# A transformer layer in fp32: the down projection of two steps as seven products of half the columns

## What is computed

```
x = fwht(x * SU_ug) / SCALE                      # Hadamard transform over 512
x_up   = x @ W_up.T   * (Wscale_ug[:INTER] * SCALE)     # 512 -> 2048
x_gate = x @ W_gate.T * (Wscale_ug[INTER:] * SCALE)
x = silu(x_gate) * x_up
x = fwht(x * SU_dp) / SCALE
x = x @ W_down.T * (Wscale_dp * SCALE)           # 2048 -> 512, "down"
x = layernorm(x_in + x)
```

## Time and profile before

| | |
|---|---|
| median of 3 runs | 1549.19 us |
| profiled execution | 1548.87 us, span 1547.1 us |
| granted clock of TensorE, mean | 0.998 |
| PE matmuls | 11744, busy 98% |
| VectorE (DVE), ScalarE (ACT), GpSimd (POOL) busy | 67%, 40%, 30% |
| attention / block 0 / blocks 1 to 7 / end | 0 to 510 / 510 to 661 / 661 to 1530 / to 1547 us |

### The profile page before, as it was taken

How to read it: one execution, slowest core, us unless ns; L and a number is a source line. 1 busy time by engine, 2 the same in 40 slices (tenths; PEclk the granted TensorE clock), 3 DMA queues, 4 the chain that set the end, 5 groups by cost and what they waited for, 6 DMA issues and landing times.

```text
span 1547.1 us, 29636 instructions
## 1 busy us (share of the span) xinstructions
PE 1513.5 (98%) x11744; PEld 1422.1 (92%) x11744; DVE 1034.0 (67%) x1790; ACT 625.8 (40%) x1289; POOL 465.0 (30%) x580
## 2 busy tenths in 40 slices
PE   6999999999999999999999999999999999999998
PEld 5977978888887899899999999999999999999998
DVE  6876787677687886865575576566467547557645
ACT  4263245236227755533333343343343333334332
POOL 5465457438338533500220030030040022003001
PEclk9999999999999999999999999999999999999999
DMA  7031122122112796678578667767776857866862
GB/s 284 1 116 69 35 83 102 35 82 103 64 64 101 275 378 246 236 273 307 205 242 295 231 241 263 268 216 264 272 238 226 322 195 257 288 231 231 283 234 97
DMA packets 92072, 307.63 MB, mean 199 GB/s; under 512 B 9888, under 2 KB 10272, under 8 KB 90144
## 3 DMA queue, kind: packets, MB, share of 16 engines
q1 hardware_dynamic: 90928, 301.54, 54.8%
q10 hardware_dynamic: 1008, 4.20, 0.7%
HBM read 255.37 MB, written 50.33 MB: 198 GB/s over the span
## 4 chain that ended last, share of the span: by engine, by line
PE 64%; DVE 4%; ACT 1%; issue 1%; POOL 1%; POOLq 0%; DVEq 0%; ACTq 0%
PE ff_bank_b L2061 16%; PE ff_bank_a L2061 11%; PE ff_bank_c L2061 11%; PE ff_acc L2095 8%; PE ff_acc L2098 7%; PE ff_acc L2086 7%; DVE ff_d_lo L1775 2%; PE ff_x_ps L2020 1%; PE ff_x_ps L2009 1%; PE ff_x_ps L2032 1%; ACT at_union L601 1%; DVE ff_c L1826 0%; DVE ff_h_lo L1794 0%; DVE ff_c L1822 0%; DVE ff_ring L1770 0%
## 5 line engine op out<-in xcount | busy, mean ns | idle before, releaser
L2061 PE MATMUL ff_bank_b<-ff_x_hi,ff_ring 128*128 128x256 f32 x1536 | 296.8, 278 | 4.1 <-DVE ff_c L1826 3.5
L2061 PEld LDWEIGHTS ff_bank_b<-ff_x_hi,ff_ring 128*128 128x128 f32 x1536 | 246.3, 188 | 5.6 <-issue 5.4
L2061 PE MATMUL ff_bank_b<-ff_x_lo,ff_ring 128*128 128x256 f32 x768 | 212.8, 277 | 0.0
L2095 PE MATMUL ff_acc<-ff_d_lo,ff_h_hi 128*128 128x256 f32 x1008 | 199.8, 279 | 2.4 <-DVE ff_d_lo L1775 2.4
L2061 PE MATMUL ff_bank_c<-ff_x_hi,ff_ring 128*128 128x256 f32 x1024 | 200.3, 280 | 0.0
L2061 PE MATMUL ff_bank_a<-ff_x_hi,ff_ring 128*128 128x256 f32 x1024 | 199.6, 279 | 0.0
L2098 PE MATMUL ff_acc<-ff_d_hi,ff_h_lo 128*128 128x256 f32 x1008 | 197.7, 277 | 0.0
L2061 PEld LDWEIGHTS ff_bank_c<-ff_x_hi,ff_ring 128*128 128x128 f32 x1024 | 164.2, 188 | 2.2 <-issue 2.2
L2061 PEld LDWEIGHTS ff_bank_a<-ff_x_hi,ff_ring 128*128 128x128 f32 x1024 | 164.3, 188 | 0.3 <-issue 0.2
L1822 DVE TENSOR_TENSOR ff_c<-ff_bank_b,ff_c 128x512 f32<-128x512 f32 x64 | 44.3, 692 | 172.0 <-PE ff_bank_b L2061 171.1
L2095 PEld LDWEIGHTS ff_acc<-ff_d_lo,ff_h_hi 128*128 128x128 f32 x1008 | 152.9, 188 | 6.4 <-issue 6.4
(11 more groups left out here) (321 smaller groups left out, 3482.3 us busy)
## 6 DMA issues: line engine op xcount, KB each, us to landing
ff_ring<-gu_scratch SPq DMA_DIRECT2D x392, 512.0 KB, 5.1
gu_scratch<-ff_ring SPq DMA_DIRECT2D x56, 512.0 KB, 4.3
at_xt<-in_xt SPq DMA_DIRECT2D x4, 2048.0 KB, 8.0
at_xn<-in_x SPq DMA_DIRECT2D x32, 256.0 KB, 2.9
x_scratch<-at_x SPq DMA_DIRECT2D x32, 256.0 KB, 2.0
ff_raw<-in_wgu SPq DMA_DIRECT2D x8, 1024.0 KB, 7.1
at_wd_a<-in_wd SPq DMA_DIRECT2D x8, 512.0 KB, 4.0
mixed_scratch<-at_wd_a SPq DMA_DIRECT2D x8, 512.0 KB, 3.3
```

Source lines behind the costliest of these rows:

```text
L2061: i = pe.matmul(bank[:, m, :], r[:, a, m, c, :], b[:, k, c, :], start=(k < 3 and m == 0 and c == 0 and b is x_hi and a == 0), stop=(m == 1 ...
L2095: pe.matmul(acc[:, t, half], h_hi[q][:, j, k], d_lo[:, j, half], start=False, stop=False, skip_group_check=True)
```

## The change

Two steps (four chunks of 128) are taken together, and the down product of them is done by Strassen-Winograd as well: h is cut into halves of tokens and odd and even chunks, `wd` into halves of its columns and odd and even chunks. Seven products (`down_product`) of 256 tokens x 256 columns x 256 inner values have 12 matmuls of 256 columns each, 84 for two steps. This holds for blocks 1 to 7 without the last two steps: `GROUPS` = 27 groups. Block 0 and the last two steps keep the old way (`whole`).

- PE: after the products of an even step p come the seven down products of the two steps before p (group q, `group_at`). After an odd step nothing comes. The banks 0, 1, 2 of `acc` are used in the order 0, 1, 2, 1, 0, 1, 2.
- The sum over the block is no longer in PSUM but in `y`: VectorE adds six times per group a bank to a quarter of y (`add_down`); product 1 (M1) is copied by ScalarE (`copy_m1`), summed over the groups by POOL (`add_m1`, not for a block's first group) and added to three quarters of y at the block's end (`close_y`).
- Tokens: POOL makes four sums of 256 elements per step (`sum_h`); ScalarE rounds and VectorE lowers four parts of h per step (`split_h`, `lower_part`), three of 512 elements and one of 256, two of them in the next step, before `product` 1.
- Weights: POOL combines the down weights once, 16 operations (`combine_down`). In each group ScalarE rounds seven operands (`split_pair`), POOL lowers five (`lower_pair`, three of them ahead), VectorE two. They share three slots.
- Statistics are taken in two parts in step 1 (`measure`). `X_AT` is moved, in part into the group (positions 12 and 15, behind down products 3 and 6). The fetch of y is issued two products after the store (n = 20, not 22). Tiles move in SBUF, some share space with those of block 0.

The core of the diff:

```diff
+        BANK_OF = (0, 1, 2, 1, 0, 1, 2)
+        READS = ((1, 0, 1), (2, 1, 1), (3, 1, 1), (4, 0, 0), (5, 1, 0), (6, 0, 1))
-        X_AT = {(4, 3): ("turn", 0), (4, 6): ("mix", 0), (4, 8): ("turn", 1), (5, 3): ("mix", 1), (5, 6): ("turn", 2),
-                (5, 8): ("mix", 2), (6, 3): ("turn", 3), (6, 6): ("mix", 3)}
+        X_AT = {(3, 6): ("turn", 0), (4, 3): ("mix", 0), (4, 6): ("turn", 1), (4, 12): ("mix", 1), (4, 15): ("turn", 2),
+                (5, 3): ("mix", 2), (5, 6): ("turn", 3), (6, 3): ("mix", 3)}
...
-                    if n == MULS * 3 + 1 and not last:
+                    if n == MULS * 2 + 6 and not last:
# POOL
+            def combine_down(g):
+                upper, lower = slice(4 * g, 4 * g + 3, 2), slice(4 * g + 1, 4 * g + 4, 2)
+                b11, b12, b21, b22 = (down_half(b, chunks) for chunks in (upper, lower) for b in range(2))
...
+            def sum_h(blk, p):
...
+                pool.wait_ge(*prod_s.now(s, 3))
+                pool.tensor_tensor(s1, a21, a22, ALU.add).then_inc(sum_s, 1)
+                pool.tensor_tensor(s3, a11, a21, ALU.subtract).then_inc(sum_s, 1)
...
+            def lower_pair(q, k):
+                n = MULS * q + k
+                pool.wait_ge(*pair_hi(n + 1))
+                pool.tensor_tensor(pair_slot(n, 1), pair_weights(q, k), pair_slot(n, 0).bitcast(F32), ALU.subtract).then_inc(b_lo, 1)
+
+            def lower_three(q):
+                for k in range(3):
+                    lower_pair(q, k)
+
+            def add_m1(q):
+                blk, g = q // 4 + 1, q % 4
+                if g == 0:
+                    return
+                pool.wait_ge(m1_copied, q + 1)
+                if g > 1:
+                    pool.wait_ge(*m1_added(blk, g - 1))
+                pool.tensor_tensor(m1_sum[:, :, :], m1_sum[:, :, :], m1[:, :, :], ALU.add).then_inc(m1_summed, 1)
+
+            def close_y(q):
...
+                for a, b, reads in ((1, 0, 0), (0, 1, 1), (1, 1, 3)):
+                    part = out[:, 2 * a:2 * a + 2, HB2 * b:HB2 * b + HB2]
+                    pool.wait_ge(*down_read(6 * q + reads))
+                    pool.tensor_tensor(part, part, m1_sum[:, :, :], ALU.add).then_inc(m1_summed, 1)
+
+            def down_group(q):
+                lower_pair(q, 3)
+                add_m1(q)
+                lower_pair(q, 5)
+                if closes(q):
+                    close_y(q)
+
+            def body(blk):
...
+                sum_h(blk, 4)
+                if blk < FBLK - 1:
+                    pair_sums(blk + 1)
+                lower_three(group_at(blk, 6))
+                sum_h(blk, 5)
+                if blk < FBLK - 1:
+                    butterfly_head(blk + 1)
+                down_group(group_at(blk, 6))
+                if blk < FBLK - 1:
+                    sum_h(blk, 6)
+                    butterfly_tail(blk + 1)
# ScalarE
+            def down_group(q, blk, p, last):
+                copy_m1(q)
+                split_pair(q, 3)
+                if not whole(blk, p):
+                    split_h(blk, p, 0)
+                split_pair(q, 4)
+                at(act, blk, p, 12, last)
+                split_pair(q, 5)
+                split_pair(q, 6)
+                at(act, blk, p, 15, last)
# VectorE
+            def add_down(q, r):
+                blk = q // 4 + 1
+                k, a, b = READS[r]
+                part = y[blk % 2][:, 2 * a:2 * a + 2, HB2 * b:HB2 * b + HB2]
...
+                dve.wait_ge(*down_mul(MULS * q + k + 1))
+                dve.tensor_tensor(part, down_bank[BANK_OF[k]], part, ALU.add).then_inc(added.sem, 1)
...
+            def down_group(q, blk, p, last):
+                add_down(q, 0)
+                if not whole(blk, p):
+                    lower_part(blk, p, 0)
+                lower_pair(q, 4)
+                add_down(q, 1)
+                add_down(q, 2)
+                lower_pair(q, 6)
+                add_down(q, 3)
+                add_down(q, 4)
+                at(blk, p, 15, last)
+                if not whole(blk, p):
+                    lower_part(blk, p, 1)
+                add_down(q, 5)
...
                 evict_m7(s)
                 at(blk, p, 3, last)
+                if not whole(*before(blk, p)):
+                    lower_part(*before(blk, p), 2)
+                    lower_part(*before(blk, p), 3)
                 product(s, p, 0, 0, bank_a[:, 1, :], sg[:, 0, 0:HB2], hf[:, 0, 0:HB2])
...
-                lower_h(s)
-                if p == 1:
-                    statistics(blk - 1, 1 - parity)
+                q = group_at(blk, p)
+                if q is not None:
+                    down_group(q, blk, p, last)
+                elif not whole(blk, p):
+                    lower_part(blk, p, 0)
+                    lower_part(blk, p, 1)
# TensorE
+            def down_product(q, k):
+                n, bank = MULS * q + k, down_bank[BANK_OF[k]]
+                if k == 0:
+                    pe.wait_ge(*hq_lo(8 * q + 8))
...
+                elif k == 4:
+                    pe.wait_ge(m1_copied, q + 1)
+                else:
+                    pe.wait_ge(*down_read(6 * q + {3: 1, 5: 3, 6: 2}[k]))
+                if k in (4, 6):
+                    pe.wait_ge(*pair_lo_v(2 * q + k // 2 - 1))
+                else:
+                    pe.wait_ge(b_lo, 5 * q + (1, 2, 3, 4, 0, 5)[k])
...
+                for m in range(2):
+                    for c in range(2):
+                        for u, v in ((0, 0), (0, 1), (1, 0)):
+                            i = pe.matmul(bank[:, m, :], h[:, c, HB2 * u + P * m:HB2 * u + P * m + P], b[:, v, HB2 * c:HB2 * c + HB2],
+                                          start=(k < 3 and m == 0 and c == 0 and u == 0 and v == 0), stop=(m == 1 and c == 1 and u == 1), skip_group_check=True)
...
-                    down(s - 1, (p - 1) % 2, p == 1, p == 0, lambda: at(p, 7))
-                    at(p, 8)
+                    q = group_at(blk, p)
+                    if q is not None:
+                        for k in range(MULS):
+                            down_product(q, k)
+                            at(p, 10 + k)
```

311 lines of the change are left out of this document (259 added, 52 removed).

## The result

The changed kernel takes 1622.7 us (median, 1621.5 to 1629.5) against 1551.7 for the kernel before in the same session: a ratio of 1.047, 95% interval [1.043, 1.051]. The forecast was 1571, with a range up to 1603. The direction was right and the size too small: 0.047 instead of 0.014 of the time. The profiled execution took 1621.9 us with a span of 1620.1; before it was 1547.1.

A forecast was written before the change was run, and what follows sets the result against it. It took the kernel as bound by PE's matmuls (98% busy). The terms -37.3 - 3.5 + 36 + 18 + 4 + 5 = +22 on 1548.9 gave 1571 us, range 1537 to 1603.

The forecast's parts named there:

- Matmuls: Over the 27 groups: 324 fewer matmuls of 256 columns on PE, saving 37.3 us.
- the old waits: At the six changes of block: PE's waits for one DVE eviction go, saving 3.5 us.
- Change of block: At six block changes: PE's fourth product waits for DVE's late eviction of product 2, 6.0 us each, +36.
- 7.0 + 1.1 + 0.7: At a block change: DVE's old work, extra lows less a half, then the eviction, 8.8 us after the last product.
- Inside the group: 20 places within groups: PE waits for DVE's low of weight 5, delayed by turns with POOL; +18 us, ends 0 and 34.
- Odd to even step: 21 places: two DVE token lows, with POOL's h sums between, precede product 2's eviction; +4 us, ends 0 and 15.
- Turns and mixings of x: On PE: the same 24 each, only moved, counted among the hidden work at no cost.
- Block 0: At its end: sixteen POOL weight sums slow DVE's operations with both inputs in SBUF; +5 us, ends 0 and 14.
- The mixture of 1.36 and 1.41: Products' two durations, in us, may change share: 11 us less if all fast, some 20 more if all slow.
- The granted clock: In blocks 1 to 7: read as 1.00 from the profile before, with no term for a fall.
- rival 3: Whole blocks: DVE and POOL saturate on shared operands and pile-ups reach PE; 1615 us, chance 0.11.
- Rival 4: In the groups: weight loads into the ring come late for fourteen products in a row; 1598 us, chance 0.05.

The follow-up runs named there:

- change_whole: The changed kernel with the down pass of a block's last two steps done as in the kernel before, 21 groups instead of 27; 1586.1 us, ratio 1.024.
- turn_in_three: The changed kernel with turn 0 of the next block's x behind the fourth product of step 3 instead of the seventh; 1615.0 us, ratio 1.042.
- sums_in_gap: change_whole plus turn 0 behind step 3's fourth product, and GpSimd's 12 W_down sums held until VectorE's last x split of block 1; 1571.6 us.
- small_sums: The changed kernel with GpSimd's sums of h (but the first step's), of M1 and into y made 8 columns wide; 1595.5 us, ratio 1.030.
- three_groups: sums_in_gap with VectorE's order in a step put by what TensorE waits for, mainly M6's eviction earlier; 1554.5 us, ratio 1.002.
- before_xs_moved: The kernel before with the gap ahead of xs_hi 64 bytes wider, so the tiles behind it, h included, stand higher; 1559.8 us, ratio 1.006.
- before_xs_alone: before_xs_moved with 64 bytes more ahead of h, so h stands at 96 modulo 128 as in the kernel before; 1544.1 us, ratio 0.992.
- before_one_wait: The kernel before with one more TensorE wait in step 1 of blocks 2 to 7, by VectorE's order alone; 1576.7 us, ratio 1.018.
- three_groups_again: The kernel three_groups run once more, unchanged, for a readable profile and a narrower interval; 1553.2 us, ratio 1.003.

## Why the prediction fell short, step by step

- *Matmuls, -37.3 and the old waits, -3.5:* right (-36.7, -4.4).
- *Change of block, +36:* right in place and nearly in size. The pauses are 29.4, and with the restarts about 32. The chain "7.0 + 1.1 + 0.7" is the one seen; 10.6 us of it came already at the first product, for the x low, where the prediction had all of it at the fourth. change_whole shows that it belongs to the change: all of it went.
- *Inside the group, +18:* 12.8 in the account, but not as told. I had 1.2 us at 20 places for DVE's low. Those waits are 13, of 0.5 us with the restart (6.5 in all). The rest stands at a group's first product (1.5), for GpSimd's lows (2.2) and, behind a mixing of x, for an addition to y (2.6). One reason may be that a product at 1.41 gives DVE 0.05 us more; no run tests it.
- *Odd to even step, +4 with ends 0 and 15:* **the step that failed**, with 28.5. It took DVE's list from the token lows on, and left out what the change had moved into the list before them: turn 0 to (3, 6) and turn 3 at (5, 6), where a covered down pass used to follow. "Turns and mixings of x, the same 24 each on PE, moved" stood among what is hidden; turn_in_three priced one of the moves at 8 us. The other part, step 2's first product (8.1), stands behind two lows of 1.7 us each, `lower_part` 2 and 3 ahead of `product`: a wait that no term had.
- *Block 0, +5 with ends 0 and 14:* 9.6 with block 1's first step (6.0 + 3.6); sums_in_gap gave 6.5 back. Too small, within its ends.
- *The mixture of 1.36 and 1.41, left out of the sum:* +15.3, within the "+20 if all were slow". It was the largest term after the failed one, and the prediction gave no reason why it should stay as it was.
- *The granted clock:* 1.00 was read off and not asked again. It fell behind the pauses at five of the seven changes: +7.4, no term. change_whole, without these pauses, has 1.6 us of it.
- The shares, from the forecast's 22 to 73: the failed step +24.5, the pace +15.3, short distances (restarts above all) +8.9, half clock +7.4, block 0 +4.6, the second step of block 1 and roundings +1.6, changes of block -6.6, groups -5.2.
- *Rivals:* rival 3 came nearest in time (1615), by its pile-ups. Its ground is true in part: narrowing GpSimd's sums gave 27 us in small_sums, by contention and by GpSimd's own time together. Its block change of 8 (4.9 measured) and its group of 1.7 (0.6) are wrong, and full exclusion was not needed: from the changed kernel to three_groups the steps are 37 us by the six groups left out, 8 by turn 0, 6 by the sums held back and 17 by DVE's order. The Trainium skill (Perfetto Trace Analysis, Optimizing Scalar/DVE Operations) has its warning of the shared port; the lows of 3.42 us agree. Rival 4 is out: no releaser is a ring load, and they land in 4.9 us.

## What to carry to other kernels

Where a cover is taken away, write down the whole list of the engine behind it from its last free moment, with what the same change moved into that list; a load of 60 to 76% says nothing of the one operation that the bound engine waits for. A saved matmul is worth its time only if the stream keeps its pace and clock: count the distances between matmuls before and after. Where they grew at the same granted clock, look at the places of the two operands in SBUF, and try 64 bytes more between them. And keep the old way at the one place where the chain is longest: six groups of 27 left out took back half of the loss.

## What the runs showed of the hardware that I had not expected

- TensorE ran at more than one pace at the same granted clock: 113.3 and 117.7 ns for a matmul of 256 columns, and 120.0 in the down passes of before_xs_moved. There h stood 64 bytes further than in before_xs_alone, the slow class held 3740 - 1729 = 2011 matmuls more, and the time was 1559.8 instead of 1544.1 us. The pair that did it are the two operands of one matmul, h (the one that is loaded) and the down weights (the one that streams). The pass took 120 ns a matmul where both start at the same place modulo 128 bytes, and could run at 113.3 where they lie 64 apart. The last pass of the kernel before agrees (119.8 at the same place, 113.9 with h moved). No other distance was tried.
- A wait or a transposition can leave TensorE in the slower pace for hundreds of matmuls (before_one_wait). Why the seven-product stream stays in it nine times in ten, with the tiles as far apart as before and 14 us of pauses, is open. Its down products can run fast: in three_groups_again nearly all of block 1 from 664 to 725 us, a group in it, went at 113.3.
- After pauses of 1.6 and 3.0 us within 8 us the granted clock was 0.79 in the next 8 us at four changes of block, and stayed at 1.00 at two with the same pauses; behind the single pause of 3.5 us in block 1 it was 0.82. Behind single pauses of 1.4 us at steps 4 and 6 of the changed kernel it stayed at 1.00.
